# Reordering one slot of a fused attention and feed-forward kernel: two places behind h's scale, gates behind the attention, four norms on Pool

## The reference

```python
q = layernorm(x); k = v = ctx                      # 8 heads of 16 features
ig, fg = gates of [q, k, v]                        # one row per head
cs = cumsum(log_sigmoid(fg))
log_D = tril(cs[s] - cs[t] + ig[t]);  D = exp(log_D - rowmax)
C = (q_h k_h^T / 4) * D
h = C / (max(|sum C|, exp(-rowmax)) + 1e-6) @ v_h
x = x + layernorm(h) * ln_scale
x = x + ffn(layernorm(x))                          # 128 -> 512 -> 512 -> 128, weights +-1, relu
```

## Time and profile before

| | us |
|---|---|
| median of 3 runs | 131.81 (131.75 to 132.53) |
| the profiled execution | 130.65 |
| its span, first to last instruction | 128.9 |

### The profile page before, as it was taken

How to read it: one execution, slowest core, us unless ns; L and a number is a source line. 1 busy time by engine, 2 the same in 40 slices (tenths; PEclk the granted TensorE clock), 3 DMA queues, 4 the chain that set the end, 5 groups by cost and what they waited for, 6 DMA issues and landing times.

```text
span 128.9 us, 3323 instructions
## 1 busy us (share of the span) xinstructions
PE 108.4 (84%) x1123; PEld 77.6 (60%) x1123; DVE 100.7 (78%) x294; ACT 74.0 (57%) x173; POOL 70.7 (55%) x143
## 2 busy tenths in 40 slices
PE   4989999993899585896898999999999979798961
PEld 4867658572555243564484674856747649586950
DVE  5786589828986999992899999999999989654541
ACT  3045885973495696227957773792694273747120
POOL 5595885187778389781675688687151333340000
PEclk9999999999658999999999999999999999999999
DMA  3645182139853838558129476674600100100101
GB/s 100 181 107 159 36 238 70 42 52 186 156 95 69 154 85 156 98 104 139 29 22 200 83 169 100 122 151 74 135 0 5 41 0 5 41 27 14 44 2 41
DMA packets 12992, 11.38 MB, mean 88 GB/s; under 512 B 2080, under 2 KB 11440, under 8 KB 12976
## 3 DMA queue, kind: packets, MB, share of 16 engines
q0 software_dynamic: 1728, 6.29, 26.8%
q1 hardware_dynamic: 10112, 4.53, 13.6%
q10 hardware_dynamic: 1136, 0.35, 1.2%
HBM read 8.94 MB, written 1.25 MB: 79 GB/s over the span
## 4 chain that ended last, share of the span: by engine, by line
PE 53%; ACT 14%; DVE 12%; issue 10%; POOL 5%; DMA 3%; SPq 1%; DVEq 0%; ACTq 0%; POOLq 0%
PE pF L455 19%; PE pS L381 9%; PE pF L434 5%; PE pO L395 4%; PE pO L402 3%; ACT dmat L594 3%; DVE h L872 3%; PE pF L366 3%; PE pG L343 3%; ACT h L645 3%; ACT oT L617 3%; DMA bias_in<-in_L_xattn_fgate_b 3%; PE pF L447 2%; POOL maxb L996 2%; POOL maxb L1001 1%
## 5 line engine op out<-in xcount | busy, mean ns | idle before, releaser
L455 PE MATMUL pF<-h,w 128*128 128x256 f16 x256 | 30.5, 273 | 1.2 <-DVE h L872 1.2
L872 DVE SCALAR_TENSOR_TENSOR h<-pF,h 128x512 f16<-128x512 f32 x32 | 21.5, 683 | 10.7 <-ACT h L645 10.6
L645 ACT ACTIVATE h<-pF 128x512 f16<-128x512 f32 x32 | 18.1, 594 | 19.9 <-PE pF L455 19.9
L455 PEld LDWEIGHTS pF<-h,w 128*128 128x128 f16 x256 | 24.5, 98 | 4.3 <-DVE h L872 1.3
L1029 POOL TENSOR_TENSOR x2p<-x,x2p 128x128 f16<-128x128 f32 x16 | 9.1, 569 | 19.0 <-ACT x2p L631 18.9
L785 DVE SCALAR_TENSOR_TENSOR cmat<-pS,dmat 128x1024 f32<-128x1024 f32 x15 | 18.2, 1215 | 1.1 <-PE pS L381 1.1
L381 PE MATMUL pS<-q_heads,qcT 64*128 64x512 f32 x64 | 19.0, 672 | 0.0
L996 POOL TENSOR_SCALAR_AFFINE_SELECT maxb<-aT 128x1024 f32<-128x1024 f32 x12 | 13.3, 1107 | 4.1 <-ACT em L575 4.1
L395 PEld LDWEIGHTS pO<-cmat,vals 128*32 128x32 f32 x256 | 6.4, 112 | 12.8 <-issue 10.3
L1001 POOL DMA_DIRECT2D maxb<-running_max x12 | 11.4, 953 | 3.6 <-POOL maxb L996 3.6
L395 PE MATMUL pO<-cmat,vals 128*32 128x128 f32 x256 | 10.5, 283 | 3.5 <-POOL vals L986 2.2
(11 more groups left out here) (124 smaller groups left out, 198.2 us busy)
## 6 DMA issues: line engine op xcount, KB each, us to landing
maxb<-running_max POOLq DMA_DIRECT2D x12, 512.0 KB, 5.2
out<-outb SPq DMA_DIRECT2D x8, 128.0 KB, 2.3
xs<-in_x SPq DMA_DIRECT2D x3, 256.0 KB, 3.3
cs_in<-in_ctx SPq DMA_DIRECT2D x3, 256.0 KB, 4.1
q_heads<-qcT SPq DMA_DIRECT2D x24, 32.0 KB, 2.7
xs<-in_x SPq DMA_DIRECT2D x2, 128.0 KB, 3.2
cs_in<-in_ctx ACTq DMA_DIRECT2D x1, 256.0 KB, 3.6
k_in<-in_L_ffn_k SPq DMA_DIRECT2D x1, 256.0 KB, 3.5
```

Source lines behind the costliest of these rows:

```text
L455: last = pe.matmul(bank[:, u], w1[:, k, columns], h1[:, k, part], start=(k == 0 and part == 0), stop=(k == FT - 1 and part == 1))
L645: act.activation(hidden(f, m, 0), ffn_place(f, m), ACT.Relu).then_inc(ffn_high, 1)
L872: dve.scalar_tensor_tensor(out=hidden(f, m, 1), in0=ffn_place(f, m), scalar=0.0, in1=hidden(f, m, 0), op0=ALU.max, op1=ALU.subtract).then_ ...
```

## The change

POOL: `norm_group(2)` leaves DVE; POOL does its four norms in the prologue, between `q_scale(8, 4)` and `q_scale(12, 4)`, and raises a semaphore of their own, xn_late, for which `turn_late_xn(2)` waits. In the loop slot 1 has no `place`, slot 2 has `place(4)` and `place(5)`, both behind `hx_scale(1)`.

PE: `gates(2)` and `gates(3)` move from the head of slots 4 and 8 to behind `turn_o` and the early feed-forward product; `turn_am(2)` and `turn_am(3)` move behind `weigh`. ACT: `gate_logs` of groups 2 and 3 move from ahead of `take_o` to behind `decay` and the early `high`; `gate_out` of groups 2 and 3 to behind `decay`. DVE: `gate_scans` of groups 2 and 3 move from ahead of the normalizer to the end of their slot, behind the centred h. Group 1's order on these three engines stays.

```diff
--- before.py
+++ after.py
@@ -175,6 +175,7 @@
         q_stats = sem("q_stats")
         q_rstd = sem("q_rstd")
         xn_ready = sem("xn_ready")
+        xn_late = sem("xn_late")
         vals_ready = sem("vals_ready")
         turned = sem("turned")
         turned_out = sem("turned_out")
@@ -324,7 +325,10 @@
                 turn_ctx(g, pG)
 
             def turn_late_xn(g):
-                pe.wait_ge(xn_ready, GB * (g + 1))
+                if g == 2:
+                    pe.wait_ge(xn_late, GB)
+                else:
+                    pe.wait_ge(xn_ready, GB * g)
                 pe.wait_ge(turned_out, 2 * g + 1)
                 turn_xn(GB * g, GB, pG)
 
@@ -502,18 +506,16 @@
                 g, k = divmod(n, GB)
                 prepare = n < B and g + 1 < NG
                 early, late = ffn_of_slot(n)
-                if prepare and k == 0 and n > 0:
-                    gates(g + 1)
                 if 0 < n < B:
                     scores(n)
                 if n == 1:
                     gates(1)
-                if prepare and k == 1 and g > 0:
-                    turn_am(g + 1)
                 if k == 3 and g + 2 < NG:
                     turn_late_ctx(g + 2)
                 if 0 <= n - 1 < B:
                     weigh(n - 1)
+                if prepare and k == 1 and g > 0:
+                    turn_am(g + 1)
                 if 2 <= n + 1 < DIRECT:
                     spread_never(n + 1)
                     spread_max(n + 1, 0)
@@ -527,6 +529,8 @@
                     turn_o(n - 1)
                 for f, m in early:
                     ffn(f, m)
+                if prepare and k == 0 and n > 0:
+                    gates(g + 1)
                 if k == 3 and g + 2 < NG:
                     turn_late_xn(g + 2)
                 for f, m in late:
@@ -668,12 +672,8 @@
                 early, late = ffn_of_slot(n)
                 for f, m in ffn_of_slot(n - 1)[1]:
                     high(f, m)
-                if prepare and k == 0 and n > 0:
-                    gate_logs(g + 1)
                 if n == 1:
                     gate_logs(1)
-                if prepare and k == 1 and g > 0:
-                    gate_out(g + 1)
                 if 0 <= n - 1 < B:
                     take_o(n - 1)
                 if k == 3 and g + 2 < NG:
@@ -686,8 +686,12 @@
                     turn_out(5, qcT[:, 1, :, 0], pO[:, :])
                 if n == 1:
                     gate_out(1)
+                if prepare and k == 1 and g > 0:
+                    gate_out(g + 1)
                 for f, m in early:
                     high(f, m)
+                if prepare and k == 0 and n > 0:
+                    gate_logs(g + 1)
                 if 0 <= n - 3 < B:
                     norm_x(n - 3)
                     x2_take_high(n - 3)
@@ -736,8 +740,8 @@
                     return
                 dve.wait_ge(q_rstd, n + 1)
                 dve.wait_ge(q_stats, n + 1)
-                if n >= 2 * GB and n % GB == 0:
-                    dve.wait_ge(turned, 3 if n // GB == 2 else 5)
+                if n == 3 * GB:
+                    dve.wait_ge(turned, 5)
                 e = n % (2 * GB)
                 dve.tensor_scalar(xn[:, e], xs[:, n], mv_q[:, n, 0:1], rs_q[:, n:n + 1],
                                   ALU.subtract, ALU.mult).then_inc(xn_ready, 1)
@@ -933,10 +937,7 @@
                     q_span(2 * GB, GB)
                     q_span(3 * GB, GB)
                 if n == 1:
-                    norm_group(2)
                     gate_scans(1)
-                if prepare and k == 0 and n > 0:
-                    gate_scans(g + 1)
                 if n >= 2:
                     norm_q(n + 3 * GB - 2)
                 if behind_2:
@@ -954,6 +955,8 @@
                     low(f, m)
                 if behind:
                     h_centred(n - 1)
+                if prepare and k == 0 and n > 0:
+                    gate_scans(g + 1)
                 if n == 3:
                     ffn_weights_0_2()
 
@@ -1070,13 +1073,19 @@
             for n in range(1, GB):
                 take_values(n)
             q_scale(2 * GB, GB)
+            pool.wait_ge(q_rstd, 3 * GB)
+            pool.wait_ge(turned, 3)
+            for n in range(2 * GB, 3 * GB):
+                pool.tensor_scalar(xn[:, n % (2 * GB)], xs[:, n], mv_q[:, n, 0:1], rs_q[:, n:n + 1], ALU.subtract,
+                                   ALU.mult).then_inc(xn_late, 1)
             q_scale(3 * GB, GB)
             for n in range(SLOTS):
                 if 0 <= n - 4 < B:
                     x2_take_low(n - 4)
                 if 0 <= n - 2 < B + 1:
                     hx_scale(n - 1)
-                place(n + LEAD)
+                for i in (() if n == 1 else (GB, GB + 1) if n == 2 else (n + LEAD,)):
+                    place(i)
                 take_values(n + GB)
```

## The result

| | before | after |
|---|---|---|
| median of 20 runs, us | 131.75 | 129.94 |
| the profiled execution | 130.65 | 129.42 |
| its span | 128.9 | 127.7 |
| POOL busy, us | 70.7 | 74.1 |

The ratio is 0.985, with a 95% interval of 0.9816 to 0.9885: 1.5% faster, about 2 us. The forecast was 128.7, so the direction is right, and 1.8 of the forecast 3.1 us came. The mean of all 20 executions is 130.9 us against 131.7.

A forecast was written before the change was run, and what follows sets the result against it. PE's own work bounds the second half, so losses in slots 2 to 7 count. -3.3 (slots 2 to 7) + 0.3 (8, 9) - 0.1 (smaller overlaps) = -3.1: from 131.81 to 128.7 us, range 126.6 to 130.6.

The forecast's parts named there:

- the forecast's own signs of being wrong: scores(4) later than 34.5, clock at 0.50, PE wait over 1 us in slots 8 to 10, first residual near 29.
- Part 1: Slot 2: hx_scale(1) before the places, at 24.95; weigh(2) at 29.8 for 32.02; second scale delayed 0.2, bounds 0 and 0.7.
- Part 2: Group 2's norms on POOL: 0.58 each, 2.3 us in all, under its wait for am_ready; path gain nothing, cost 0.
- Part 3: Slot 4: scores(4) at 33.2 for 37.35, 4.1 us earlier, behind the q_heads transfers; scores(5) at 37.7, 3.4 earlier.
- It is hidden: Rival, chance 0.10: two places' transfers delay the last heads to 35.6, scores(4) only 1.7 earlier, slots 8 and 9 take the rest; 131.6.
- Part 4: Slots 4 to 7: f_ln at 39.1, no gain; make_c(5) at 41.7 for 45.00; first product's second low 3.3 us earlier.
- Part 5: Slots 8 and 9: -0.2 from moved gates and logs, +0.5 from late place(12); together +0.3, ends -0.3 and +1.5.
- the clock still falls: Rival, chance 0.18: new idle times lower PE's clock in slots 4 and 5, gain only 1.7 us, time 130.1.
- The port pair: DVE beside POOL's affine_selects: two norms take 0.79 instead of 0.28; more caught work, an estimated 1 us less gain.
- The other side: Rival, chance 0.06: late gate_out holds POOL at place(8) and place(12), PE waits; at worst +5.4, time 134.1.

The follow-up runs named there:

- only_pool: The kernel before with only POOL's places and the norms as changed, gates, logs and scans as before: ratio 0.9873 to the kernel before.
- only_order: The kernel before with only the changed order of PE, ACT and DVE, POOL's list and the norms as before: ratio 1.0018 to the kernel before.
- norms_on_dve: The changed kernel with the four norms of group 2 back on DVE in slot 1: ratio 0.9878 to the kernel before.
- places_late: The changed kernel with place(8) moved to slot 6 and place(12) to slot 10, behind hx_scale: ratio 0.9885 to the kernel before.
- places_apart: The changed kernel with place(5) moved to slot 3, in front of place(6): ratio 0.9885 to the kernel before.
- filler: The changed kernel with 36 matmuls that compute nothing on PE ahead of scores(4), about 2.5 us: ratio 0.9946 to the kernel before.
- gate_out_early: The changed kernel with gate_out of groups 2 and 3 ahead of decay in slots 5 and 9: ratio 0.9831 to the kernel before.
- heads_first: The changed kernel with SP issuing group 1's eight head transfers before the store of its running maximum: ratio 1.0103 to the kernel before.

## Why the prediction was right or wrong

The time lay inside the stated range. The path in front of it was right up to weigh(2); three of the forecast's own signs of being wrong also came: scores(4) later than 34.5, a clock of 0.50, and a wait of PE over 1 us in slots 8 to 10. Part of the agreement in the median is not the forecast's doing: it took the median as 1.16 above the profiled execution, and behind the change it was 0.52. Profile against profile, 1.2 of 3.1 us came.

**Part 1, h's scale first: right, nearly to the tenth.** ve_hx at 25.01 (25.0 forecast), the residual at 26.43 to 27.04 (26.5 to 27.15), hatt to 29.11 (29.1), weigh(2) at 29.71 (29.8). The delay of the second scale was mis-sized, beyond its upper bound of 0.7: the residual of slot 3 starts at 32.16, where DVE was free for it at 31.18 and 31.3 was forecast; the two places took 2.28 us each instead of 2.0 (the second select 1.38 instead of 1.1), and the vals copy behind them 0.6 instead of 0.3. only_pool and only_order show that POOL's part, the places and the norms together, carries the gain as far as the ratios tell. norms_on_dve has the places without the norms' move, and its ratio isn't told from the change's, which points to the places.

**Part 2, the norms: right on the path, wrong in the price.** 0.83 each instead of 0.58, 3.33 in all. The cover was almost used up.

**Part 3, scores(4) at 33.2: wrong for this execution.** It was 35.12. The forecast is 33.2 - 17.9 = 15.3 behind scores(1), and places_late, with the same list up to there, has 15.29. In the profiled executions with two places back to back scores(4) started 15.3 to 18.2 behind scores(1), so the forecast took one landing for a thing that varies by 3 us. The heads' longest landings were 4.4 to 4.7 us in the three profiles with the places apart (before, only_order, places_apart) and 4.3 to 6.8 us in the eight with them together and the heads issued as before. That points to the second place's transfer, as the rival "It is hidden" had it, but doesn't show it. That rival was wrong about the price: with the heads 2 us earlier, places_late is only 0.6 us earlier at scores(7).

**Part 4, make_c(5) at 41.7: the step that failed.** It came at 43.45, 1.55 earlier than before and not 3.3. places_late has make_c(5) at 25.0 behind scores(1) with no other wait in the way, where the forecast stands at 41.7 - 17.9 = 23.8. Of these 1.2 us, 0.9 are there at the normalizer (hatt at 22.2 for 39.2 - 17.9 = 21.3). Two terms make them. The sum left out DVE's three conversions, which cost nothing under a wait before and put DVE's residual of slot 4 0.8 us behind POOL's scale now. And POOL's scale itself is 0.5 us later than the forecast residual (ready at 19.4 for 36.8 - 17.9 = 18.9), with the second place's delay of Part 1 ahead of it in POOL's list. Some of it came back, since the norm of slot 4 took 0.37 us instead of the forecast's 0.79; the residual took 0.75 beside the select instead. The other 0.3 is the centred h, which the forecast's sum leaves out between its start at 40.1 and the scans. This splitting is read from the rows; no run had the conversions away and the heads early.

The remaining 0.6 of the changed kernel goes with late heads and the low clock: it has f_ln ready at 41.70 and DVE waits 0.46 us for it, where the forecast had it at 39.1, a microsecond ahead of the scans, and places_late has no such wait. filler, with late heads and a clock that holds, doesn't lose these 0.6 either.

**Part 5, slots 8 and 9: the mechanism right, both terms larger.** Forecast -0.2 and +0.5. From scores(7) to scores(10) the change gains 0.5 more, and the place held by the late am_ready costs 1.11 at turn_x2(6) instead of 0.5. The sum from scores(7) to scores(11) is +0.17; forecast +0.3. gate_out_early, which moves nothing but gate_out, takes the wait to 0.27, so it is the late am_ready; of the 0.84 us less waiting, 0.5 are left at scores(11).

**The clock.** The rival "the clock still falls" gave 130.1, close to the 129.94 measured, and the clock did fall, behind 3.06 us of idle PE. But filler's profiled execution, where it doesn't, is 0.7 us shorter to scores(7), not 1.4: half of this agreement is an accident.

**The port pair.** The norm of slot 3 took 0.93 us, 32.76 to 33.69, beside the select of 32.52 to 33.61, where the norm of slot 2 took 0.33. The rule of the Trainium skill on the port pair (SBUF — State Buffer, "SBUF: two separate sides"), which the forecast put beside its norms, agrees with that. The 2.27 us in norms_on_dve are not explained by the selects alone: that norm began 0.8 us ahead of the select it ran beside.

**The other side.** The mechanism is real: POOL waits 2.06 us for em ahead of place(8) and 2.44 ahead of place(12), and PE then 2.15 and 1.11 us for x2p. Its price is far from 5.4 us: 0.7 are lost between scores(10) and scores(11), and little in slot 6, where places_late takes the wait away without a gain.

## What to carry to other kernels

When a stall goes, list again every instruction of the engine that waited in it, between the stall's place and the next wait: work that was free under the old wait (here 1.3 us of weight conversions) can come onto the path the moment the wait is gone, up to where the next wait takes over (here 0.8 us). In an in-order queue, what has to be moved is whatever waits for the latest event, behind the urgent work; but two such pieces in a row hand a delay to the next slot (0.99 us in slot 3 here, 1.15 in slot 11 of places_late). A half of a change that gains nothing alone (only_order) can hide in a good total: run the halves. And before one execution's row is read as a cause, look at the same row in the other executions: the wait at scores(4) was 1.1 us in places_late and 4.1 in gate_out_early, two kernels that are the same up to there.

## What the runs showed of the hardware that was not expected

**The prologue is not constant.** Between executions scores(1) starts at 17.8 to 20.8 us with nearly the same instructions ahead of it. One difference is PE's speed: the first eight gate products take 0.43 us in the changed kernel and 0.66 in filler, where the 32 gate products run from 9.10 to 11.03 instead of 8.53 to 9.61. 0.66 is also what eight of them took at the granted clock of 0.50 in the earlier trace rows, yet the page's clock row reads full speed in the prologue in both. The six profiled executions with 0.66 have scores(1) at 18.8 to 20.8, the eight with 0.43 at 17.8 to 18.0, but for places_late (18.8). (PE's timelines, the changed kernel, then filler.)

```profile
8.53 0.43 PE L347 MATMUL pG<-qcT,wkv 128*32 128x128 f32 x8
```

```profile
9.10 0.66 PE L347 MATMUL pG<-qcT,wkv 128*32 128x128 f32 x8
```

**Equal transfers land at very different times.** The eight head transfers of one group, all alike, landed 2.0 to 5.9 us after their issue in the changed kernel's profile, the last ones beside the transfers of two places, and up to 6.8 in gate_out_early. In heads_first, issued before any place, all eight landed after 2.0.

**One norm on DVE took nearly seven times as long beside POOL.** The norm of 2.27 us above takes 0.34 by itself (0.28 each in a row of four). In the changed kernel the same norm began beside the same issue of place(4) (27.29 for 27.22) and took 0.33, so what held it is open.
